# A float32 product done as three one-pass products of high and low parts, in a local transformer layer

## The reference, cut to what matters

```python
def ffn_layer(x, g, bln, W1, b1, W2, b2):
    mu = x.mean(-1, keepdims=True)
    var = ((x - mu) ** 2).mean(-1, keepdims=True)
    xn = (x - mu) / jnp.sqrt(var + 1e-05) * g + bln
    hg = xn @ W1 + b1                       # the up product: 128 -> 2 x 341
    a, gate = jnp.split(hg, 2, -1)
    return a * jax.nn.gelu(gate, approximate=False) @ W2 + b2

for i in range(DEPTH):                      # DEPTH = 6
    x = attn_layer(shift_tokens(x), Wqkv[i], q_scale[i], k_scale[i], Wo[i]) + x
    x = ffn_layer(shift_tokens(x), ln_g[i], ln_b[i], W1[i], b1[i], W2[i], b2[i]) + x
```

## Time and profile before

| | |
|---|---|
| time, median of 3 runs | 2600.63 us (2596.15 to 2601.51) |
| the profiled execution's own time | 2589.45 us |
| its span | 2587.7 us |
| PE matmul busy | 2448.3 us (95%) |
| PE weight load busy | 1973.1 us (76%) |
| DVE busy | 2154.9 us (83%) |
| ACT busy | 2033.9 us (79%) |
| POOL busy | 1519.4 us (59%) |

### The profile page before, as it was taken

How to read it: one execution, slowest core, us unless ns; L and a number is a source line. 1 busy time by engine, 2 the same in 40 slices (tenths; PEclk the granted TensorE clock), 3 DMA queues, 4 the chain that set the end, 5 groups by cost and what they waited for, 6 DMA issues and landing times. The chain is left out here.

```text
span 2587.7 us, 118567 instructions
## 1 busy us (share of the span) xinstructions
PE 2448.3 (95%) x52349; PEld 1973.1 (76%) x52349; DVE 2154.9 (83%) x2455; ACT 2033.9 (79%) x4077; POOL 1519.4 (59%) x1029
## 2 busy tenths in 40 slices
PE   6799999999999999999999999699999999997999
PEld 2488888888888888888888887467776776775787
DVE  5888888888888888888888886389898988885898
ACT  4689888898889899898998886667676766664776
POOL 3788888888888888887898784122222222222110
PEclk9899999999999999999999999799999999999999
DMA  3234433443444344334443332123232322221221
GB/s 99 56 93 95 108 78 93 94 110 83 97 94 110 83 96 99 95 85 98 103 100 82 86 83 59 45 46 69 45 73 48 67 47 66 51 58 30 83 74 41
DMA packets 275793, 202.01 MB, mean 78 GB/s; under 512 B 117568, under 2 KB 215880, under 8 KB 274248
## 3 DMA queue, kind: packets, MB, share of 16 engines
q1 hardware_dynamic: 275280, 194.42, 31.3%
HBM read 36.96 MB, written 1.11 MB: 15 GB/s over the span
## 5 line engine op out<-in xcount | busy, mean ns | idle before, releaser
L514 POOL TENSOR_TENSOR lt_t_sin<-lt_qk,lt_tab 128x512 f32<-128x512 f32 x384 | 683.3, 1801 | 222.2 <-DVE lt_qk L1298 220.1
L519 POOL TENSOR_TENSOR lt_qr<-lt_qr,lt_t_sin 128x1024 f32<-128x1024 f32 x192 | 457.7, 2384 | 28.2 <-POOL lt_t_sin L514 0.9
L2082 DVE TENSOR_REDUCE fa_neg_max<-bank 128x1 f32<-128x1024 f32 x256 | 301.6, 1220 | 91.2 <-PE bank L1879 89.7
L2004 ACT ACTIVATE fa_prob<-bank,fa_neg_max 128x1024 f32<-128x1024 f32 x128 | 142.6, 1114 | 216.5 <-DVE fa_neg_max L2082 164.2
L1905 PE MATMUL bank<-fa_prob_t,fa_v 32*64 32x128 f32 x16384 | 293.6, 276 | 16.5 <-issue 11.8
L1905 PEld LDWEIGHTS bank<-fa_prob_t,fa_v 32*64 32x64 f32 x16384 | 244.4, 130 | 78.0 <-issue 58.1
L2092 DVE STREAM_TRANSPOSE fa_prob_t<-fa_prob 128x1024 f32<-128x1024 f32 x256 | 302.1, 1219 | 0.0
L607 PE MATMUL bank<-lt_w_high,lt_x_high 128*128 128x512 f32 x576 | 262.3, 455 | 0.8 <-ACT lt_v_tok L1011 0.4
L979 ACT COPY lt_qk<-bank 128x512 f32<-128x512 f32 x384 | 224.3, 589 | 23.7 <-PE bank L609 2.8
L1298 DVE TENSOR_TENSOR lt_qk<-lt_qk,lt_rn 128x2048 f32<-128x2048 f32 x96 | 239.8, 2498 | 2.4 <-ACT lt_rn L1005 2.2
L1291 DVE TENSOR_REDUCE lt_ssq<-lt_qr 128x32 f32<-128x2048 f32 x96 | 218.9, 2280 | 25.6 <-ACT lt_qr L987 25.6
(11 more groups left out here) (260 smaller groups left out, 5853.1 us busy)
## 6 DMA issues: line engine op xcount, KB each, us to landing
lt_v<-lt_v_tok SPq DMA_DIRECT2D x576, 128.0 KB
fa_v<-fa_v_tok SPq DMA_DIRECT2D x256, 128.0 KB, 2.7
lt_v<-lt_v_tok SPq DMA_DIRECT2D x192, 64.0 KB
lt_k_t<-lt_k_t SPq DMA_DIRECT2D x84, 128.0 KB, 2.9
lt_v<-lt_v SPq DMA_DIRECT2D x168, 64.0 KB, 2.0
lt_w_raw<-in_lt_wqkv_dram SPq DMA_DIRECT2D x36, 256.0 KB, 3.6
ex_cw_all<-cw_kept SPq DMA_DIRECT2D x8, 1024.0 KB, 4.6
lt_x_s<-h_in SPq DMA_DIRECT2D x96, 64.0 KB, 2.7
```

The source lines that it names most:

```text
L514: pool.tensor_tensor(dst[:, :, i, :], src[:, :, 1 - i, :], tab[:, g // 2 % 2, 1, at:at + 32].unsqueeze(1).to_broadcast([P, HEADS, 32]), AL ...
L519: pool.tensor_tensor(qr[:, g % 2, half], qr[:, g % 2, half], t_sin[:, :], ALU.add).then_inc(S.rotated, 1)
L2082: dve.tensor_reduce(neg_max[:, u % 2, par:par + 1], bank[:, 2 * par:2 * par + 2, :].rearrange("p a n -> p (a n)"), AX.X, ALU.max, negate=T ...
```

## The change

The up product is made of high and low parts. ACT's bias step now writes the rounded high part `f_high` straight away (the same instruction as before with another output). DVE then makes the low part `f_low` from `f_norm`, the bias and `f_high` (`norm_low`, new), and PE waits for `f_low` instead of for ACT. PE makes 18 `float32r` matmuls for a chunk instead of 6 plain ones. Once a layer, in step `16 layer + 4`, ACT rounds the whole of `w_1` (682 columns, `split_up_high`) and POOL subtracts (`split_up_low`).

To make room, `w_1` gets one buffer instead of two, and the angle tables are fetched by two DMAs for each chunk (`load_tab`) into two buffers instead of all at the start. The load of layer 0's `w_1` moves from the start to step 0, since the time mixing's weights now lie in the single buffer.

```diff
 def load_layer(layer, i):
     r = layer % 2
-    if i == 0 and layer >= 2:
+    if i == 0 and layer >= 1:
+        sp.wait_ge(S.w_1_low, layer)
+    if i == 1 and layer >= 2:
         sp.wait_ge(S.ff_out, BLOCKS * (layer - 1))
...
+def load_tab(c):
+    if c >= 2:
+        sp.wait_ge(S.tab_scaled, c - 1)
+    sp.dma_start(tab_raw[:, c % 2, 0, :], A["cos"][:, c % BLOCKS, :]).then_inc(s_tab[c % 2], 16)
+    sp.dma_start(tab_raw[:, c % 2, 1, :], A["sin"][:, c % BLOCKS, :]).then_inc(s_tab[c % 2], 16)
...
+def split_up_low(layer):
+    pool.wait_ge(S.w_1_high, layer + 1)
+    pool.tensor_tensor(w_1_low[:, :], w_1[:, :], w_1_high[:, :].bitcast(F32), ALU.subtract)\
+        .then_inc(S.w_1_low, 1)
...
 def up(c, j):
-    r, m = c // BLOCKS % 2, FROWS[j]
+    m = FROWS[j]
     if j == 0:
-        pe.wait_ge(S.f_normed, c + 1)
+        pe.wait_ge(S.f_low, c + 1)
+        if c % BLOCKS == 0:
+            pe.wait_ge(S.w_1_low, c // BLOCKS + 1)
     wait_free(pe, "up", c, j)
-    o = bank[0:m, turn_bank("up", c, j), :]
-    pe.matmul(o[:, 0:PAIR], w_1[:, r, FF + j * P:FF + j * P + m], f_norm[:, :], start=True, stop=True)
-    pe.matmul(o[:, PAIR:2 * PAIR], w_1[:, r, j * P:j * P + m], f_norm[:, :], start=True, stop=True)\
-      .then_inc(S.up, 1)
+    for half, lo in enumerate((FF + j * P, j * P)):
+        o = bank[0:m, turn_bank("up", c, j), half * PAIR:half * PAIR + PAIR]
+        pe.matmul(o, w_1_high[:, lo:lo + m], f_high[:, :], start=True, stop=False)
+        pe.matmul(o, w_1_low[:, lo:lo + m], f_high[:, :], start=False, stop=False)
+        mm = pe.matmul(o, w_1_high[:, lo:lo + m], f_low[:, :], start=False, stop=True)
+    mm.then_inc(S.up, 1)
...
 # ACT, shift_norm(c)
-act.activation(f_norm[:, :], f_norm[:, :], ACT.Identity, bias=lvec[:, layer % 2, 1:2])\
-   .then_inc(S.f_normed, 1)
+if c >= 1:
+    act.wait_ge(S.up, FB * c)
+act.activation(f_high[:, :], f_norm[:, :], ACT.Identity, bias=lvec[:, layer % 2, 1:2])\
+   .then_inc(S.f_high, 1)
...
+def split_up_high(layer):
+    wait_layer(act, layer)
+    if layer >= 1:
+        act.wait_ge(S.up, FB * BLOCKS * layer)
+    act.copy(w_1_high[:, :], w_1[:, :]).then_inc(S.w_1_high, 1)
...
+def norm_low(c):
+    dve.wait_ge(S.f_high, c + 1)
+    if c >= 1:
+        dve.wait_ge(S.up, FB * c)
+    dve.scalar_tensor_tensor(out=f_low[:, :], in0=f_norm[:, :], scalar=lvec[:, c // BLOCKS % 2, 1:2],
+                             in1=f_high[:, :].bitcast(F32), op0=ALU.add, op1=ALU.subtract).then_inc(S.f_low, 1)
...
 # DVE, in the loop over the steps
     if live(i):
         shift_scores(i, 0)
+    if even(i, 5) is not None:
+        norm_low(even(i, 5))
```

More of the change, by code:

```diff
@@ L90, in time_mixing_and_local @@
         w_o = buf("w_o", [P, 2, PAIRS, P])
-        w_1 = buf("w_1", [P, 2, 2 * FF])
+        w_1 = buf("w_1", [P, 2 * FF])
+        w_1_high = buf("w_1_high", [P, 2 * FF], F32R)
+        w_1_low = buf("w_1_low", [P, 2 * FF], F32R)
         w_2 = buf("w_2", [P, 2, FB, P])
@@ L125, in time_mixing_and_local @@
         f_norm = buf("f_norm", [P, PAIR])
+        f_high = buf("f_high", [P, PAIR], F32R)
+        f_low = buf("f_low", [P, PAIR], F32R)
         f_gate = buf("f_gate", [P, FB, PAIR])
@@ L132, in time_mixing_and_local @@
         STAT = 7
-        names = ("tables mask w_even w_odd layer_even layer_odd scale_even scale_odd cast cleared k_cleared tab_scaled x_even x_odd "
+        names = ("tab_even tab_odd mask w_even w_odd layer_even layer_odd scale_even scale_odd cast cleared k_cleared tab_scaled x_even x_odd "
                  "staged_first staged_high staged w_high w_low look v_even v_odd klook_even klook_odd f_x "
@@ L137, in time_mixing_and_local @@
                  "turned turn_out scores rowmax shifted probs rowsum inv_sum prob_turned prob_out av av_out "
-                 "att_turned att_out out out_done f_mean f_squared f_var f_ln f_rstd f_scaled f_normed up gated "
+                 "att_turned att_out out out_done f_mean f_squared f_var f_ln f_rstd f_scaled f_high f_low w_1_high w_1_low up gated "
                  "hidden down ff_out last_x last_mean last_squared last_var last_ln last_rstd last_scaled last_out").split()
@@ L201, in time_mixing_and_local @@
         wmod = rows(v_tok[:, :, :, :].rearrange("p a b n -> p (a b n)")[:, 0:2 * 6 * P], 2)
-        tm_w = rows(w_1[:, 1, 0:5 * P], 5)
+        tm_w = rows(w_1[:, 0:5 * P], 5)
         group_mean_w, g_center, g_mix = (w_2[:, 1, i, :] for i in range(3))
@@ L253, in splits_at, with up_split_at @@
             return ks
+        def up_split_at(i):
+            return i // SLOTS if i % SLOTS == 4 and 0 <= i < ALL else None
         def wait_place(eng, k):
@@ L426, in _ @@
                     load_scale(0, n)
-                sp.dma_start(tab_raw[:, :, 0, :], A["cos"]).then_inc(S.tables, 16)
-                sp.dma_start(tab_raw[:, :, 1, :], A["sin"]).then_inc(S.tables, 16)
-                for n in range(4):
+                load_tab(0)
+                load_tab(1)
+                for n in range(1, 4):
                     load_layer(0, n)
@@ L444, in _ @@
                         load_x(even(i, -5))
+                        load_tab(even(i, -5))
                     if live(i + 2) and has_look(i + 2):
@@ L452, in _ @@
                     for layer in range(1, LAYERS):
+                        if i == 0 and layer == 1:
+                            sp.wait_ge(T.o, NCH)
+                            load_layer(0, 0)
                         n = i - (SLOTS * layer - 11)
@@ L469, in _ @@
                 sp.wait_ge(T.w, 48)
-                sp.wait_ge(S.tables, 32)
                 sp.wait_ge(S.mask, 16)
@@ L558, in _ @@
                     add_bias(n)
-                pool.wait_ge(S.tables, 32)
                 scale_tables(0)
@@ L597, in _ @@
                         scale_tables(c)
+                    if up_split_at(i) is not None:
+                        split_up_low(up_split_at(i))
             @blk.tensor
@@ L1219, in _ @@
                             split_high(k)
+                    if up_split_at(i) is not None:
+                        split_up_high(up_split_at(i))
                     if live(i - 1) and even(i - 1, 5) is not None:
@@ L1353, in norm @@
                     if c >= 1:
-                        dve.wait_ge(S.up, FB * c)
+                        dve.wait_ge(S.f_high, c)
+                        dve.wait_ge(S.f_low, c)
                     dve.scalar_tensor_tensor(out=f_norm[:, :], in0=bank[:, STAT, 0:PAIR], scalar=lvec[:, layer % 2, 0:1],
                                              in1=f_rstd[:, :], op0=ALU.mult, op1=ALU.mult).then_inc(S.f_scaled, 1)
+                def norm_low(c):
[4 more added lines that the diff above has]
+                                             in1=f_high[:, :].bitcast(F32), op0=ALU.add, op1=ALU.subtract).then_inc(S.f_low, 1)
                 def hidden(c, j):
```

9 lines of the change are left out of this document (6 added, 3 removed).

## The result

| | before | after |
|---|---|---|
| median | 2598.39 us (2595.04 to 2601.51, 4 runs) | 2632.18 us (2629.86 to 2636.88, 4 runs) |
| the profiled execution's own time, span | 2589.45, 2587.7 us | 2630.48, 2628.7 us |

The ratio is 1.0132, 95% interval 1.0119 to 1.0146: slower by 1.3%, 34 us, where 2638 (2611 to 2664) was forecast.

The account below looks back on a forecast made before the run. PE was taken as the bound, busy 1182.6 of 1200 us. Chunk waits 27.6, last three chunks 1, ACT's rounding 4.5, POOL's subtraction 7.8, less 3 absorbed, make 37.9 us; on the 2600.63 median, 2638 us (2611 to 2664).

Parts of the forecast that it names:

- The mechanism: On DVE, `norm_low` is held until POOL's rotation addition ends, ends 0.29 us behind it, and PE starts 0.06 us later.
- The up product: On PE, eighteen one-pass matmuls 0.12 us apart take 2.25 us instead of 2.68, plus 0.10 for the open weight load.
- ordinary chunk: One of 33 among the first 45 chunks; a chunk costs x + 0.02 us, 27.6 us over all 45.
- x: How far POOL's rotation addition ends behind the first up matmul's start before the change; mean 0.56 us in ordinary chunks.
- the absorbing rival: PE absorbs the wait or POOL's addition ends ahead of `norm_low` in most chunks: 2607 to 2612, 2615 at most; chance 0.12.
- Once a layer: ACT's rounding of `w_1` costs 0.75 us a layer, 4.5 in all; POOL's subtraction 1.3 us a layer, 7.8 in all.
- Absorption: PE's unnamed stops of 28.7 us may shrink where PE now waits anyway; 3 us allowed.
- The sum: All terms over the whole kernel: 27.6 + 1 + 4.5 + 7.8 - 3 = 37.9 us, giving 2638 us.
- The faster rival: `norm_low` is not held by POOL, PE wins 18 us less 12 once a layer: -6 us, 2595; chance 0.06.
- What was put at nothing: The angle-table DMAs on SP, the `w_1` fetches and `f_high` on ACT were said to cost nothing.
- The signs: `norm_low` near 1.6 us, PE waiting some 35 us in about 40 chunks, later second row maximum, exponents' wait up 0.75 us.

Follow-up runs that it names:

- a1_psum: The changed kernel with the scaled norm kept in PSUM, so `norm_low` reads one wide SBUF input instead of two; 2592.45 us, ratio 0.9957 to the kernel before.
- a3_halves: The changed kernel with POOL's last addition of each rotation issued as two instructions of 512 columns; 2620.48 us, ratio 1.0072 to the kernel before.
- a4_one_split: The changed kernel with `w_1` split for layer 0 only, layers 1 to 5 using layer 0's parts; 2620.6 us, ratio 1.0062 to the kernel before.

## Why the prediction was right, point by point

- **The mechanism** stood as told: POOL's last addition holds `norm_low`, which ends 0.28 to 0.29 us behind it (0.29 from the earlier trace rows), and PE starts 0.06 us later. a1_psum and a3_halves show it as cause, not only as coincidence. By the Trainium skill, "SBUF — State Buffer", section "SBUF: two separate sides", a DVE instruction with two SBUF inputs is kept out for the whole of a GpSimd instruction; the runs agree, with a median of 1.55 us with two such inputs and 0.47 with one.
- **The up product**: 0.12 us from start to start and 2.33 us in all with the open weight load, as forecast (2.25 + 0.10). The Trainium skill's formula ("TensorE: Matmul & The Clock Gate", Back-to-back issue gap), which it gives for a single matmul, would have had 109 ns; the row's 0.12 held.
- **The cost of an ordinary chunk was sized over a third too high.** My sum has for the table's 40 chunks 24.5 us (27.6 x 40/45). Taking the splits away (a4_one_split) leaves +31.0 - 14.3 = 16.7 us at this place; counting only the distance ahead of up, which grew by 32.0, it is 17.7. Read from before, x was 0.59 us on average. In a4_one_split it is 32.0/40 - 0.29 - 0.06 = 0.45: L545 ends less far behind the place where PE would have started. A likely reason is that PE is late as a whole while POOL's addition starts from earlier products, the absorbing rival at a small scale; no run tests that.
- **Once a layer**: ACT's rounding cost 0.6 us a layer ahead of L691 where 0.75 was put. POOL's part was 6.5 us for five layers, and the wait ahead of up has 6.0 for them. The terms together were 10.3 for five layers; measured are 6.2 (trace), 12 (medians) or 18 us (ratios), so their sum is neither confirmed nor refuted.
- **Absorption**: I allowed 3 us. Beside the wait (38.4 us ahead of up), the up product and the scores, all products together took 3.1 us less in 40 chunks: of that size, and also of the spread's.
- **The sum**: in 40 chunks 24.5 + 10.3 - 2.5 = 32.3 us were forecast and 22.9 came. Outside these, where the sum had 5.6 us, 11.5 came (the last product of the local transformer starts 34.4 us later): 2.5 us are there before the first scores and 3.9 appear at chunk 0. A small sum inside and a large one outside meet near the forecast: 34 us by the medians for 38. That the total came so near is in part luck. What the 2.5 us are I didn't test; a4_one_split, the same code up to there, has 0.5.
- **The faster rival** was priced well: "not held", 2595; with the hold taken away it is 2592 (a1_psum).
- **What was put at nothing**: in 300 to 1500 us neither PE nor its weight load waits for a DMA in the changed kernel.
- **The signs** named: norm_low's mean near 1.6 us (1.68 in the window), PE's wait some 35 us in about 40 chunks (39.1 in 45). The second row maximum started 3.46 us behind the start of `norm` (828.24 against 824.78) where it was 1.80. The wait for the exponents grew by 0.6 us, not by 0.75.

## What to carry to other kernels

Before giving DVE an instruction with two SBUF inputs whose result PE needs soon, look at what GpSimd runs at that time, and count from the end of that instruction; one input left in PSUM, or GpSimd's work in shorter instructions, takes the wait away or shortens it. A wait for an engine that idles elsewhere is dear only where the bound engine waits: the same hold cost 41 us with PE waiting and at most 0.4% without. And before moving small products together on TensorE, look at how far apart their runs are, and at when the transfers of the instruction queue end.

## What the runs showed of the hardware beyond that

Runs of 128 products with 128 weight loads (11 ns a pair) stopped for up to 3 us in the second run when it was 2.6 us from the last product of the one to the first of the other, 28 to 31 us more than before in 40 chunks, and hardly (about 5 us) at 4.3 us and more. Stops over 0.2 us in such runs ended 1.16 to 1.65 us behind the end of a 16384-byte transfer of the instruction queue, in 328 of 328 cases. Further, products of 256 columns behind such a stop came 0.21 us apart instead of 0.12. Plain float32 products of this size take 2.68 us for six where 18 one-pass products take 2.24: three products of parts took 16% less than one plain one.
